# Cross-attention and FFN block on one core: where the feed-forward weights are converted, when they are loaded, and two early norms that read their root from PSUM

## Chip, cores, metric

The kernel runs on one core of one Trainium2 chip. The metric is device time in microseconds (us) of one execution. Three timed runs of the kernel before gave 454.68, 455.16 and 455.61 us; the median is 455.16.

## What is computed

Sixteen batches of 128 tokens and 512 features go through one cross-attention (32 query heads of 16, 8 groups of keys and values, so four query heads share a group) with a residual, and then a gated feed-forward in fp8 with a residual.

```python
def xattn(q, kv, Wq, Wk, Wv, Wfc, bfc):
    qh = heads(q @ Wq.T, 32)                    # q = layernorm(x)
    kh, vh = repeat(heads(kv @ Wk.T, 8), 4), repeat(heads(kv @ Wv.T, 8), 4)
    attn = softmax(qh @ kh.T / 4, axis=-1)
    return (attn @ vh) @ Wfc.T + bfc
def ffn(x, w_gating, w_linear):                 # operands cast to e4m3, results bf16
    return q8(gelu(q8(x) @ q8(w_gating[0])) * (q8(x) @ q8(w_gating[1]))) @ q8(w_linear)
x = x + xattn(layernorm(x), ctx, ...)
x = x + ffn(layernorm(x), ...)
```

`w_gating` is 2 x 512 x 2048 and `w_linear` 2048 x 512, both fp32 in memory. Before a matmul may use them they have to be clamped to +-240 and written as fp8.

## The kernel before

**Stages.** The batches go in eight pairs, p = 0 to 7 (`NB = 2`). Each pair has a softmax stage and an "up" stage. The softmax stage is a loop over slots n = 0 to 19: in slot n TensorE (PE) makes the transposed scores of tile n (L557, 16 tiles), ScalarE (ACT) takes two exponentials of them (`p`, L838, fp32, and `phi`, L841, fp16), GpSimd (POOL) subtracts (`plo`, L1277), and three slots later PE weighs the values with `plo` and `phi` (L577, L579). Between these, the same slots prepare pair q = p + 1: keys, values, the first norm `xn` (L1034), its transposition by PE (L497), the query projection (L451 to L453) and its split `cq` (ACT L824, VectorE (DVE) L1002). The up stage has eight units k = 0 to 7. It finds the row maxima of the next pair (PE L528, then DVE L1070), for p = 0 it runs the output projection of batch 0 (`bank<-wfc,aoT`), and for p >= 1 it runs the gating matmuls of pair p - 1 (L649) with their gelu and copy on ACT (L860, L864), product and fp8 clamp on DVE (L1126, L1136). The second norm `xn2` is L1120.

**What fills a tile by DMA.** The projected queries and keys are restacked by DMA: `qs<-cq` (L381, and L904 from ACT's queue in the first pair), `ks<-khl` (L367), `kmask<-khl` (L359), and the rows of maxima `qs<-mrow` (L387, and L893 from ACT's queue). The transposed scores wait for them. SP issues nearly all DMAs, in the order of its program; it stands still where a load has to wait for its place.

**The weights.** All weights are 29 chunks c of 512 KB: 0 to 4 are those of the attention, 5 to 20 the gating weights, 21 to 28 the linear ones. `W_PLACE` names the place into which chunk c is loaded (three stage buffers, `x4`/`x6` = rows of the residual's ring not yet used, `l`, `g` = the room of fp8 tiles that are written later). A chunk is converted in one of two ways: by one DVE instruction (L1016, the chunks in `W_DVE`, in the slots of `DVE_SLOTS`), or by a clamp on POOL (L1297) and a cast on ACT (L779), in the slots of `CLAMP_SLOTS` (cast two slots later) and the units of `CLAMPS_UP` (cast one unit later). `W_LOADS` says at which of four points of SP's program in p = 0 and p = 1 a chunk is loaded: after `kmask`, after the keys, the context and x, after the queries, and after the rows of maxima of the next pair.

```python
W_DVE = [7, 8, 9, 17, 18, 19, 20, 21, 22]
CLAMP_SLOTS = ((10,), ())
DVE_SLOTS = ((3, 6, 9), (2, 4, 6, 8, 11, 13))
CLAMPS_UP = (tuple(range(6)), (0, 1, 2, 4, 5, 6))
W_LOADS = (((), range(12, 18), (), range(18, 21)), ((), range(21, 26), range(26, CHUNKS), ()))
```

Every engine works through its own program in order, with semaphores between them. From pair 2 on no chunk is left, and a pair takes the same time as every other.

## Time and profile before

| | us |
|---|---|
| runs | 454.68, 455.16, 455.61 |
| profiled execution | 456.79 |
| its span | 454.80 |
| busy: PE, DVE, ACT, POOL | 424.9, 330.5, 313.8, 239.8 |
| mean granted TensorE clock | 0.966 of full speed |

```profile
## 2 busy tenths in 40 slices
PE   6887889799899999999999999999999998999997
PEld 6755756577677778787877778787877785568783
DVE  4776578888987589767897689758987676666351
ACT  6845958685798747974697748974698647865450
POOL 5575996694639702883168603983178502950000
PEclk9966958899999999999999999999999999999999
DMA  8894598286503370145303460236203330000001
```

One digit is the busy share of 11.4 us in tenths; PEclk is the TensorE clock granted. The first softmax stage lies in slices 3 to 6, its up stage in 6 and 7, the second pair in 7 to 11. After that the pattern repeats. Start times in the rows are us from the start of the span.

### The profile page before, as it was taken

The page shows a single profiled execution, that of the slowest core. Times are in us where ns is not written, and L with a number is a line of the kernel's source. Part 1 is how long each engine was busy: PE and PEld are TensorE (multiplying, and loading weights), DVE is VectorE, ACT ScalarE, POOL GpSimd, SP SyncE. Part 2 cuts the span into 40 slices and gives each one's busy share as a digit, 9 for nine tenths or more (in the row PEclk, how much of TensorE's full clock was granted, in tenths as well). Part 3 has the DMA queues.
Part 4 walks back from the last instruction along what each step waited for, and adds up shares of the span by engine and source line. Part 5 has one row for each costly group of instructions (what it writes and reads, how often), then busy time and mean ns, then how long its engine had stood idle before and what let it go on. Part 6 is the DMA issues. An engine that isn't in the chain of part 4 may idle for free.

```text
span 454.8 us, 9696 instructions
## 1 busy us (share of the span) xinstructions
PE 424.9 (93%) x3596; PEld 329.1 (72%) x3596; DVE 330.5 (73%) x687; ACT 313.8 (69%) x576; POOL 239.8 (53%) x228
## 2 busy tenths in 40 slices
PE   6887889799899999999999999999999998999997
PEld 6755756577677778787877778787877785568783
DVE  4776578888987589767897689758987676666351
ACT  6845958685798747974697748974698647865450
POOL 5575996694639702883168603983178502950000
PEclk9966958899999999999999999999999999999999
DMA  8894598286503370145303460236203330000001
GB/s 277 305 251 163 146 340 234 66 303 143 188 1 89 94 190 4 43 123 117 95 5 95 114 163 1 67 101 156 56 20 100 76 88 3 25 25 1 2 25 69
DMA packets 21231, 49.66 MB, mean 109 GB/s; under 512 B 4672, under 2 KB 5184, under 8 KB 21184
## 3 DMA queue, kind: packets, MB, share of 16 engines
q1 hardware_dynamic: 20828, 48.22, 37.2%
q10 hardware_dynamic: 356, 0.82, 0.6%
q8 instruction: 29, 0.48, 0.5%
q14 instruction: 18, 0.15, 0.1%
HBM read 23.86 MB, written 4.19 MB: 62 GB/s over the span
## 4 chain that ended last, share of the span: by engine, by line
PE 69%; DVE 15%; POOL 6%; ACT 4%; issue 3%; DMA 2%; ACTq 1%; POOLq 0%; DVEq 0%
PE bank L649 21%; PE bank L668 11%; PE bank L451 7%; PE bank L452 6%; PE bank L453 6%; PE bank L557 5%; DVE mneg L1070 4%; POOL plo L1277 4%; PE bank L528 4%; PE bank L486 2%; PE bank L577 2%; PE bank L579 2%; DMA qs<-cq 2%; DVE osum L1083 2%; PE bank L497 1%
## 5 line engine op out<-in xcount | busy, mean ns | idle before, releaser
L1277 POOL TENSOR_TENSOR plo<-p,phi 128x512 f16<-128x512 f32 x128 | 152.6, 1204 | 70.3 <-ACT phi L841 69.5
L649 PE MATMUL bank<-x2T,wgate 128*128 128x256 fp8e4 x1024 | 125.1, 273 | 0.0
L649 PEld LDWEIGHTS bank<-x2T,wgate 128*128 128x128 fp8e4 x1024 | 94.7, 98 | 22.0 <-issue 5.6
L1070 DVE TENSOR_REDUCE mneg<-bank 128x4 fp32r<-128x512 f32 x128 | 84.5, 684 | 16.1 <-PE bank L528 15.9
L838 ACT ACTIVATE p<-bank 128x512 f32<-128x512 f32 x128 | 77.6, 606 | 21.2 <-PE bank L557 20.3
L841 ACT ACTIVATE phi<-bank 128x512 f16<-128x512 f32 x128 | 77.5, 605 | 0.0
L864 ACT CAST ff<-bank 128x512 bf16<-128x512 f32 x64 | 37.5, 585 | 46.0 <-PE bank L649 46.0
L528 PE MATMUL bank<-kmask,cq 128*128 128x512 f32 x128 | 60.1, 495 | 4.6 <-DVE mneg L1070 3.0
L668 PE MATMUL bank<-wlin,act 128*128 128x512 fp8e4 x224 | 64.3, 378 | 0.0
L557 PE MATMUL bank<-qs,ks 98*128 98x512 f32 x128 | 55.3, 432 | 4.5 <-ACT phi L841 2.4
L860 ACT ACTIVATE gate<-bank 128x512 bf16<-128x512 f32 x64 | 38.2, 597 | 26.0 <-PE bank L649 25.9
L577 PEld LDWEIGHTS bank<-vt,plo 128*128 128x128 f16 x512 | 32.1, 98 | 28.9 <-issue 19.1
L577 PE MATMUL bank<-vt,plo 128*128 128x49 bf16 x512 | 45.9, 190 | 2.1 <-POOL plo L1277 1.2
L579 PE MATMUL bank<-vt,phi 128*128 128x49 bf16 x512 | 43.9, 186 | 0.0
L451 PE MATMUL bank<-cx,wq 128*128 128x256 f32 x112 | 39.8, 356 | 0.8 <-DVE cx L1002 0.8
L1126 DVE TENSOR_TENSOR prod<-gate,ff 128x512 bf16<-128x512 bf16 x64 | 30.2, 472 | 13.1 <-ACT ff L864 13.1
L1261 POOL TENSOR_TENSOR cx<-cin,cx 128x512 fp32r<-128x512 f32 x14 | 18.1, 1296 | 38.6 <-ACT cx L788 38.6
L1256 POOL TENSOR_TENSOR rstd<-var,half_neg 128x1 f32<-128x1 f32 x16 | 9.1, 569 | 55.3 <-DVE var L1113 55.3
L1083 DVE TENSOR_REDUCE osum<-bank 128x128 f32<-128x384 f32 x64 | 35.7, 557 | 2.2
L451 PE MATMUL bank<-wfc,aoT 128*128 128x512 f32 x64 | 31.5, 493 | 3.8 <-DVE aoT L1002 3.7
L579 PEld LDWEIGHTS bank<-vt,phi 128*128 128x128 f16 x512 | 33.4, 98 | 0.0
L528 PEld LDWEIGHTS bank<-kmask,cq 128*128 128x128 f32 x128 | 25.1, 201 | 10.3 <-DVE mneg L1070 6.6
(117 smaller groups left out, 823.1 us busy)
## 6 DMA issues: line engine op xcount, KB each, us to landing
qs<-cq SPq DMA_DIRECT2D x90, 128.0 KB, 2.4
stage<-in_w SPq DMA_DIRECT2D x15, 512.0 KB, 6.7
ks<-khl SPq DMA_DIRECT2D x96, 64.0 KB, 2.0
cin<-in_ctx SPq DMA_DIRECT2D x8, 512.0 KB, 4.1
xr<-in_x SPq DMA_DIRECT2D x16, 256.0 KB, 3.2
out<-xr SPq DMA_DIRECT2D x16, 256.0 KB, 2.5
raw_l<-in_w SPq DMA_DIRECT2D x4, 512.0 KB, 8.9
raw_g<-in_w SPq DMA_DIRECT2D x4, 512.0 KB, 9.6
```

The costliest lines, as they stand in the source:

```text
L451: pe.matmul(out, a[1], b[0], start=first, stop=False)
L528: pe.matmul(bank_of("S", q, i, s)[:, :], cq[:, 0, j, tok(i)], kmask[:, 2 * half:2 * half + 2, :, tok(i)], start=True, stop=True).then_inc( ...
L557: pe.matmul(T[n % 2][:, :], ks[rows, p % 2, g // 2, g % 2, tok(i)], qs[rows, g // 2, :, tok(i)], start=True, stop=True).then_inc(st_done, 1)
L577: pe.matmul(out, plo[:, (TILES * p + n) % PBUF, j * SEQ:(j + 1) * SEQ], vt[:, p % 2, i, g, :], start=True, stop=False)
L579: mm = pe.matmul(out, phi[:, (TILES * p + n) % PBUF, j * SEQ:(j + 1) * SEQ], vt[:, p % 2, i, g, :], start=False, stop=True)
L649: mm = pe.matmul(out[:, h * TOK:(h + 1) * TOK], wgate8[:, UH * v + h, kk, part, :], x2T[:, pair, kk, :], start=kk == 0, stop=kk == KT - 1)
L668: mm = pe.matmul(lin_bank(b)[:, :], act_tile(b // NB)[:, h, b % NB, :], wlin8[:, h, :], start=h == 0, stop=h == HT - 1)
L838: act.activation(p32[:, e % P32BUF, :], T[n % 2][:, :], ACT.Exp, scale=QUARTER).then_inc(p32_ok, 1)
L841: act.activation(phi[:, e % PBUF, :], T[n % 2][:, :], ACT.Exp, scale=QUARTER).then_inc(phi_ok, 1)
L1070: dve.tensor_reduce(dst[:, :, 2 * half:2 * half + 2, j].rearrange("p a r -> p r a"), bank_of("S", q, i, s)[:, :].rearrange("p (r a k) -> p ...
L1083: dve.tensor_reduce(osum[:, b, :].rearrange("p (h d) -> p h d", h=UHEADS), o[:, :, 0:VPARTS * HD].rearrange("p h (a d) -> p h d a", a=VPARTS),
L1277: pool.tensor_tensor(plo[:, e % PBUF, :], p32[:, e % P32BUF, :], phi[:, e % PBUF, :], ALU.subtract).then_inc(plo_ok, 1)
```

## The change

It is in five parts, all of them before pair 2.

1. The loads of chunks 7 to 11 wait on SP until all four parts of the first queries are stacked, and the DMA of the second batch's row maxima is issued between the third and the fourth of them.
2. In the first softmax stage DVE converts six chunks (7 to 12, in slots 5, 6, 7, 8, 9, 11) where it was three (slots 3, 6, 9); POOL and ACT still convert one, in slot 12 where it was slot 10. In the first up stage POOL and ACT convert five where it was six, in the second four (units 1, 2, 4, 5) where it was six (0, 1, 2, 4, 5, 6). DVE converts six in the second softmax stage, as before.
3. Chunks 12 to 14 are loaded right behind `kmask`; 21 and 22 only when the row maxima of pair 1 have landed (`m_stacked[0]`); 25 to 28 all behind the queries and x of pair 1's part of SP's program (25 was ahead of the queries).
4. For the first norm of pairs 1 and 2, and the second norm of batches 0 and 1, DVE first copies the root to a PSUM bank and takes it from there, by scalar_tensor_tensor in place of tensor_scalar.
5. PE's output projection of batches 0 and 1 waits until the norms of the pair whose root lies in its bank are done. DVE's first conversion of a linear chunk waits for places l0 and l1.

```diff
-W_PLACE += ["st0", "st1", "st2", "l0", "g0", "g1", "st0", "st1", "l1"]
-W_PLACE += ["st2", "x6", "st0", "st1", "st2", "st0", "st1", "st2"]
-W_DVE = [7, 8, 9, 17, 18, 19, 20, 21, 22]
+W_PLACE += ["st0", "st1", "st2", "x6", "l0", "g0", "g1", "l1", "st0"]
+W_PLACE += ["st1", "st2", "x6", "st0", "st1", "st2", "st0", "st1"]
+W_DVE = [7, 8, 9, 10, 11, 12, 19, 20, 21, 22, 23, 24]
-CLAMP_SLOTS = ((10,), ())
-DVE_SLOTS = ((3, 6, 9), (2, 4, 6, 8, 11, 13))
-CLAMPS_UP = (tuple(range(6)), (0, 1, 2, 4, 5, 6))
-W_LOADS = (((), range(12, 18), (), range(18, 21)), ((), range(21, 26), range(26, CHUNKS), ()))
+CLAMP_SLOTS = ((12,), ())
+DVE_SLOTS = ((5, 6, 7, 8, 9, 11), (2, 4, 6, 8, 11, 13))
+CLAMPS_UP = (tuple(range(5)), (1, 2, 4, 5))
+W_LOADS = ((range(W_FREE, 15), range(15, 21), (), range(21, 23)), ((), range(23, 25), range(25, CHUNKS), ()))
...
+        def root2(b):
+            return chain_banks(b)[1][:, NB:NB + 1]
...
             stack_q(0, PAIRS - 1)
+            for hp in range(PAIRS):
+                sp.wait_ge(q_stacked[hp], 16 * 3)
             for c in range(W_GATE + W_AHEAD, W_FREE):
+                if c == W_GATE + W_AHEAD + STAGES:
+                    stack_max(0, 1)
                 load_chunk(c)
...
+                if p == 0:
+                    sp.wait_ge(m_stacked[0], 32)
                 for c in W_LOADS[p][3] if p < 2 else ():
...
+                    if b < NB:
+                        pe.wait_ge(xn_ok, NB * (b + 2))
                     pe.wait_ge(aoT_lo, b + 1)
...
+                    root = G[q - 1][:, 0:NB]
+                    if i == 0:
+                        dve.wait_ge(*((aoT_lo, NB) if q == 2 else (max_ok, TILES)))
+                        dve.tensor_copy(root, rstd1[:, :]).then_inc(root1_ok, 1)
+                        dve.wait_ge(root1_ok, q)
+                    dve.scalar_tensor_tensor(xn[:, i, :], x0, mv1[:, i, 0:1], root[:, i:i + 1].broadcast_to([P, D]),
+                                             ALU.subtract, ALU.mult).then_inc(xn_ok, 1)
...
+                    dve.tensor_copy(root2(b), rstd2[:, i:i + 1]).then_inc(root2_ok, 1)
+                    dve.wait_ge(root2_ok, b + 1)
+                    dve.scalar_tensor_tensor(xn2[:, :], xr[:, b % RING, :], mv2[:, i, 0:1], root2(b).broadcast_to([P, D]),
+                                             ALU.subtract, ALU.mult, saturate=False).then_inc(xn2_ok, 1)
```

Line numbers move with the change: the DVE conversion is L1016 before and L1031 after, the norms L1034 and L1059, POOL's clamp L1297 and L1328, `plo` L1277 and L1308, a load of a chunk L338 and L341.

**SP's queue between the first queries and the keys of pair 1** (`xr`, `raw_l`, `raw_g`, `stage` are places of chunks). Before:

```order
L381 DMA qs<-cq 32x1024 x6
L338 DMA xr<-in_w 128x1024
L338 DMA raw_l<-in_w 128x1024
L338 DMA raw_g<-in_w 128x1024 x2
L338 DMA raw_l<-in_w 128x1024
L387 DMA qs<-mrow 2x16x128
L359 DMA kmask<-khl 32x512 x4
L367 DMA ks<-khl 32x512 x12
```

After:

```order
L384 DMA qs<-cq 32x1024 x6
L341 DMA xr<-in_w 128x1024
L341 DMA raw_l<-in_w 128x1024
L341 DMA raw_g<-in_w 128x1024
L390 DMA qs<-mrow 2x16x128
L341 DMA raw_g<-in_w 128x1024
L341 DMA raw_l<-in_w 128x1024
L362 DMA kmask<-khl 32x512 x4
L341 DMA stage<-in_w 128x1024 x3
L370 DMA ks<-khl 32x512 x12
```

The row maxima have passed two loads, and three stage loads now stand ahead of the keys.

**DVE in the middle of the first softmax stage** (`bank<-rstd` is the copy of the root, `wgate` a converted chunk). Before:

```order
L1034 TENSOR_SCALAR xn<-xr,mv,rstd 128x512 x2
L1016 TENSOR_SCALAR wgate<-xr 128x1024
L1002 TENSOR_TENSOR cx<-bank,cx 128x4x128
L1081 RECIPROCAL bank<-bank 128x8
L1083 TENSOR_REDUCE osum<-bank 128x128
L1002 TENSOR_TENSOR cx<-bank,cx 128x4x128
L1093 TENSOR_TENSOR ao<-osum,bank 128x128
L1016 TENSOR_SCALAR wgate<-raw_l 128x1024
```

After:

```order
L1057 COPY bank<-rstd 128x2
L1059 SCALAR_TENSOR_TENSOR xn<-xr,mv,bank 128x512 x2
L1014 TENSOR_TENSOR cx<-bank,cx 128x4x128
L1106 RECIPROCAL bank<-bank 128x8
L1108 TENSOR_REDUCE osum<-bank 128x128
L1014 TENSOR_TENSOR cx<-bank,cx 128x4x128
L1118 TENSOR_TENSOR ao<-osum,bank 128x128
L1031 TENSOR_SCALAR wgate<-xr 128x1024
L1031 TENSOR_SCALAR wgate<-raw_l 128x1024
```

The first conversion has left the place ahead of the split of `cx`, and stands with the second behind the first `ao`.

**POOL in the second up stage** (`plo` ends the softmax stage, `cx` is the split of a later pair's context). Before:

```order
L1277 TENSOR_TENSOR plo<-p,phi 128x512 x7
L1297 TENSOR_SCALAR stage<-stage 128x1024
L1285 TENSOR_TENSOR xr<-xr,bias 128x512 x2
L1256 TENSOR_TENSOR rstd<-var,half_neg 128x1
L1297 TENSOR_SCALAR stage<-stage 128x1024
L1261 TENSOR_TENSOR cx<-cin,cx 128x512
L1297 TENSOR_SCALAR stage<-stage 128x1024
L1261 TENSOR_TENSOR cx<-cin,cx 128x512
L1297 TENSOR_SCALAR stage<-stage 128x1024 x3
```

After:

```order
L1308 TENSOR_TENSOR plo<-p,phi 128x512 x7
L1316 TENSOR_TENSOR xr<-xr,bias 128x512 x2
L1287 TENSOR_TENSOR rstd<-var,half_neg 128x1
L1328 TENSOR_SCALAR stage<-stage 128x1024
L1292 TENSOR_TENSOR cx<-cin,cx 128x512
L1328 TENSOR_SCALAR stage<-stage 128x1024
L1292 TENSOR_TENSOR cx<-cin,cx 128x512
L1328 TENSOR_SCALAR stage<-stage 128x1024 x2
```

The first clamp now is that of chunk 25, directly behind the root of the second norm; before it was the second of the stage, and of chunk 24.

## Rows read from the trace of the kernel before

**Rows 1.** Windows by stage: us, busy by engine (instructions), PEclk, DMA share, GB/s

```profile
29.26:74.83 45.57, 38.48 (x265) 29.56 (x266) 29.63 (x61) 33.47 (x56) 33.08 (x31) 0.73 0.76 228
74.83:130.59 55.76, 49.52 (x437) 39.52 (x436) 49.72 (x96) 41.84 (x77) 36.06 (x32) 0.97 0.53 163
180.90:231.30 50.40, 49.90 (x448) 39.30 (x446) 39.81 (x85) 36.44 (x70) 26.87 (x25) 1.00 0.33 85
```

**Rows 2.** Chain of waits from 24 to 132 us: start, us, what

```profile
28.59 7.41 DMA qs<-cq
...
71.74 3.27 DVE mneg L1070 x5
...
80.29 2.03 DVE xn L1034 x2
...
82.92 1.29 DVE xn L1120
```

**Rows 3.** Timeline of PE, 34 to 65 us: start, us, what [idle before <- releaser]

```profile
36.05 0.50 PE L557 MATMUL bank<-qs,ks 98*128 98x512 f32 x1 [1.90 <-DMA qs<-cq]
36.38 1.65 PE L486 MATMUL bank<-wv,cx 128*128 128x256 f32 x8
...
39.40 1.12 PE L497 MATMUL bank<-ident,xn 128*128 128x128 f32 x4 [0.59 <-DVE xn L1034]
...
62.39 1.05 PE L595 MATMUL bank<-ident,ao 128*128 128x128 f32 x4
```

**Rows 4.** Timeline of SP's queue

```profile
27.68 0.59 SPq L338 DMA_DIRECT2D xr<-in_w  x1
...
58.04 11.58 SPq L381 DMA_DIRECT2D qs<-cq  x12
...
113.79 5.12 SPq L338 DMA_DIRECT2D stage<-in_w  x3
```

**Rows 5.** Timeline of POOL and ACT in the first softmax stage

```profile
42.85 1.16 POOL L1277 TENSOR_TENSOR plo<-p,phi 128x512 f16<-128x512 f32 x1 [2.04 <-ACT phi L841]
...
44.59 1.62 POOL L1277 TENSOR_TENSOR plo<-p,phi 128x512 f16<-128x512 f32 x1
...
48.20 4.99 POOL L1277 TENSOR_TENSOR plo<-p,phi 128x512 f16<-128x512 f32 x4
...
60.18 1.04 POOL L1297 TENSOR_SCALAR raw_l<-raw_l 128x1024 f32<-128x1024 f32 x1
...
54.22 1.06 ACT L779 ACTIVATE wgate<-raw_g 128x1024 fp8e4<-128x1024 f32 x1 [0.36 <-POOL raw_g L1297]
```

**Rows 6.** Windows of 3.4 us, columns as in rows 1

```profile
53.70:57.10 3.40, 1.99 (x22) 1.13 (x20) 1.42 (x4) 3.04 (x7) 3.01 (x4) 1.00 0.94 289
57.20:60.60 3.40, 3.35 (x36) 2.18 (x36) 3.30 (x9) 3.38 (x5) 3.40 (x4) 0.50 0.95 324
...
81.00:84.40 3.40, 1.48 (x21) 1.01 (x18) 3.40 (x5) 1.27 (x4) 2.62 (x2) 1.00 0.20 49
84.50:87.90 3.40, 3.21 (x17) 2.52 (x18) 2.92 (x8) 2.24 (x5) 1.85 (x2) 0.50 0.37 87
```

**Rows 7.** DMA to landing of the `qs<-cq` transfers (L381) issued from 58.0 to 59.2

```profile
DMA to landing us min/median/max: 9.6/9.7/12.2
```

**Rows 8.** Timeline of DVE: operations with a PSUM operand, and a conversion

```profile
42.45 0.20 DVE L1081 RECIPROCAL bank<-bank 128x8 f32<-128x8 f32 x1
...
77.11 0.67 DVE L1107 TENSOR_TENSOR xr<-xr,bank 128x512 f32<-128x512 f32 x1
...
84.47 0.68 DVE L1016 TENSOR_SCALAR wgate<-stage 128x1024 fp8e4<-128x1024 f32 x1
```

**Rows 9.** Timeline of the second up stage: DVE, ACT, POOL

```profile
114.46 1.49 DVE L1126 TENSOR_TENSOR prod<-gate,ff 128x512 bf16<-128x512 bf16 x1
...
116.04 0.60 ACT L860 ACTIVATE gate<-bank 128x512 bf16<-128x512 f32 x1
...
118.47 1.08 POOL L1297 TENSOR_SCALAR stage<-stage 128x1024 f32<-128x1024 f32 x1 [0.22 <-DMA stage<-in_w]
```

More of the change, by code:

```diff
@@ L242, in xattn_ffn_kernel @@
         aoT_done, aoT_hi, aoT_lo, fc_done = sem("aoT_done"), sem("aoT_hi"), sem("aoT_lo"), sem("fc_done")
-        x1_ok, stat2, mv2_ok, var2_ok, rstd2_ok, xn2_ok, x2T_done, x2T_ok = (
+        x1_ok, stat2, mv2_ok, var2_ok, rstd2_ok, xn2_ok, x2T_done, x2T_ok, root1_ok, root2_ok = (
             sem("x1_ok"), sem("stat2"), sem("mv2_ok"), sem("var2_ok"), sem("rstd2_ok"), sem("xn2_ok"),
-            sem("x2T_done"), sem("x2T_ok"))
+            sem("x2T_done"), sem("x2T_ok"), sem("root1_ok"), sem("root2_ok"))
         gate_done, ff_done, ff_ok, gelu_ok, prod_ok, act_ok = (
@@ L414, in _ @@
                 downs = down_slots(p)
-                stack_max(p, 1)
+                if p:
+                    stack_max(p, 1)
                 if q < NP:
@@ L1015, in chunk @@
                 dve.wait_ge(*chunk_in(c))
+                if c == W_LIN:
+                    for name in ("l0", "l1"):
+                        dve.wait_ge(*chunk_free(last_of(name)))
                 dve.tensor_scalar(chunk_fp8(c), chunk_place(c), FP8_MAX, -FP8_MAX, ALU.min, ALU.max,
@@ L1033, in norm_apply @@
                     dve.wait_ge(xT_done, NB * (q - 1) + i + 1)
-                dve.tensor_scalar(xn[:, i, :], xr[:, (NB * q + i) % RING, :], mv1[:, i, 0:1], rstd1[:, i:i + 1],
-                                  ALU.subtract, ALU.mult).then_inc(xn_ok, 1)
+                x0 = xr[:, (NB * q + i) % RING, :]
+                if q == 0 or q > 2:
+                    dve.tensor_scalar(xn[:, i, :], x0, mv1[:, i, 0:1], rstd1[:, i:i + 1],
+                                      ALU.subtract, ALU.mult).then_inc(xn_ok, 1)
+                else:
+                    root = G[q - 1][:, 0:NB]
[4 more added lines that the diff above has]
+                    dve.scalar_tensor_tensor(xn[:, i, :], x0, mv1[:, i, 0:1], root[:, i:i + 1].broadcast_to([P, D]),
+                                             ALU.subtract, ALU.mult).then_inc(xn_ok, 1)
             def context_low(q, h):
@@ L1119, in norm2_apply @@
                     dve.wait_ge(x2T_done, b)
-                dve.tensor_scalar(xn2[:, :], xr[:, b % RING, :], mv2[:, i, 0:1], rstd2[:, i:i + 1],
-                                  ALU.subtract, ALU.mult, saturate=False).then_inc(xn2_ok, 1)
+                if b >= NB:
+                    dve.tensor_scalar(xn2[:, :], xr[:, b % RING, :], mv2[:, i, 0:1], rstd2[:, i:i + 1],
+                                      ALU.subtract, ALU.mult, saturate=False).then_inc(xn2_ok, 1)
+                else:
+                    dve.tensor_copy(root2(b), rstd2[:, i:i + 1]).then_inc(root2_ok, 1)
+                    dve.wait_ge(root2_ok, b + 1)
+                    dve.scalar_tensor_tensor(xn2[:, :], xr[:, b % RING, :], mv2[:, i, 0:1], root2(b).broadcast_to([P, D]),
+                                             ALU.subtract, ALU.mult, saturate=False).then_inc(xn2_ok, 1)
             def product(u):
```

## The prediction

> **What bounds the kernel now.** I read the windows by stage first. A pair without conversions takes 50.40 us, with PE busy 49.90 of it at full clock; the first pair's 45.57 us have PE busy only 38.48, at a mean clock of 0.73, and the second pair takes 55.76 us [rows 1]. PE bounds the rest of the run, where nothing is changed, so whatever the change brings or costs lies before 130.6 us and reaches the end one for one. Then the chain of waits from 24 to 132 us. With the timelines beside it, it shows five places that the change touches. (a) The second part of the queries, issued at 28.59, lands 7.41 us later [rows 2]; PE stands idle 1.90 us for it [rows 3]. SP began five chunk loads at 27.68, in the middle of that transfer [rows 4]. (b) From 42.85 on POOL's `plo` is the chain, 1.16 us each, with a clamp among them. ACT's cast at 54.22 waited for that clamp and holds ACT for 1.06 us [rows 5]; the split of the queries comes after it, and PE, which needs the split for its scores, is busy only 1.99 of 3.40 us [rows 6]. (c) Behind that gap the granted clock falls from 1.00 to 0.50 [rows 6], which is from 2.4 to 1.2 GHz, and the clock line of the page has it low in the slices up to about 71 us, over PE's out-projection. (d) At 80.29 two norms take 2.03 us and at 82.92 one takes 1.29, DVE's last work before PE may go on [rows 2]. (e) In the second up stage a product on DVE takes 1.49 us beside POOL's clamps [rows 9].
>
> **Part 1, the held loads.** With no chunk in the queue I expect the query DMAs to land by PE's need, so the 1.90 us of idle go. The value projection behind it ran at half clock, 1.65 us for eight [rows 3]; with the idle gone PE may be at full clock there and in the transposition (1.12 us). I take half of the projection's possible 0.8, because ACT's two exponentials end no earlier, and half of 1.12 for the transposition, 0.5. Part 4 takes some back: the norm that starts this step (two operations at about half a microsecond each) becomes a copy of 0.20 and operations of 0.67, by the nearest rows with a PSUM operand [rows 8], +0.35 to the first. Sum -1.9 - 0.4 - 0.5 + 0.35 = **-2.4** at POOL's `plo` of 42.85. Both ends: 0, if the queries themselves are the traffic, and -3.0.
>
> **Part 2, conversions.** In the part where POOL is the chain, two DVE conversions became dear for it: one `plo` took 1.62 in place of 1.16 (+0.46), and four took 4.99 in place of 4.64 (+0.35) [rows 5]. Now there are six, so four more at 0.4: +1.6. Below, nothing, if they fall into gaps; above, the whole 0.68 that a conversion takes by itself [rows 8], 4 x 0.68 = 2.7. I take 0.4, since it is the same pair of instructions side by side. The clamp stays one, but in slot 12, so the idle of 0.4 that POOL had behind ACT's cast goes. POOL, done at 60.18 [rows 5], is then done at 60.2 - 2.4 + 1.6 - 0.4 = 59.0. The last weighing, reciprocal, sum and division (0.4 + 0.2 + 0.55 + 0.3) put PE's turn of the output at 60.4, where it was 62.39 [rows 3]: **-2.0**. DVE comes out about there too: its split of the queries no longer waits for a cast of 1.06, which gives its last 7.6 us of work a start 2.4 + 1.0 earlier, less the delay that POOL passes on.
>
> The Trainium skill's page "Advanced Engine Details and Errata" (VectorE Performance Modes, Mode Summary) speaks against this part: the second SBUF port of VectorE is shared with GpSimd, and two-port VectorE instructions and GpSimd's block each other. Read as a full block it gives the upper end, +2.7; the `plo` rows show about 60% of that.
>
> **The clock in the first up stage.** PE's idle in the window from 53.7 was the wait for the split. Without it the fall at 57.2 should not come at that place. The out-projection at full clock would shorten the 12.6 us from the turn (62.39) to the end of the maxima (71.74 + 3.27) by 3.4 us, since DVE waits for PE's scores there. That is not free to reach the end: the query DMAs of pair 1 need 9.6 to 12.2 us to land, on DMA engines that are full (share 0.94 and 0.95 from 53.7 to 60.6) [rows 6, 7]. Their order and start hardly move (SP at 58.04 [rows 4], now about 57.8). The first pair of tiles needs three of them, issued by 59.2 and landed by 71.4 at the latest, where the stage began at 74.83 [rows 1]. Through the keys and their split the norms then move by at most 2.1 us more. But a pause of its own follows the turn (ACT and DVE split it before PE projects), and windows with some such idle did lower the clock [rows 6]. Ends 0 and -2.1; I take **-1.0**, a fall that comes one or two windows later. One cast fewer (six to five) costs and gives nothing here: DVE and DMA end last.
>
> **Part 4, second pair.** The two norms of 2.03 become 0.20 + 2 x 0.60 = 1.4 (PSUM operations of 0.67 follow each other every 0.60), the one of 1.29 becomes 0.15 + 0.65 = 0.8: -1.1. A conversion between them lay in a gap of POOL's at 0.68; shifted, it may take 0.2 more. **-0.9**, ends 0 and -1.2. PE's out-projection of batch 1 now waits for these norms, 0.65 us later; behind it stands the next scores tile. PE is idle for more than that before the transposition that follows (1.48 busy of 3.40 [rows 6]), which covers it; without that cover it would cost its 0.65. The clock was at half from 84.5 to 87.9, behind a stretch with PE busy 1.48 of 3.40 us [rows 6]; with 0.9 less of that idle it may hold. Ends 0 and -1.2, taken **-0.3**, the idle being only half gone. `plo` loses one blocked neighbour: **-0.2**.
>
> **Part 3, the second up stage.** Chunk 25 was loaded ahead of the queries. Now it is the first of the loads behind them. The load that stood there, issued at 113.79, was what POOL waited for before its clamp of 118.47 [rows 4, 9]. So in the old time frame the clamp of chunk 25 runs 118.5 to 119.5, behind it on POOL the context and all other clamps; its cast stands on ACT ahead of the gelu of unit 3, which ran at 116.04 [rows 9] and comes to 119.5 + 1.0 + 0.55 = 121.1, 5.0 later. PE may run two units ahead of ACT, and two casts are gone from ACT. Its work from 121.1 on is five gelus, five copies, a transposed tile and the maxima, 5.8 us, three casts, 3.0, and the table load and first exponential's start, 1.4: 131.3, where the next stage began at 130.59 [rows 1]. For DVE's tail I add 0.2. On the other side DVE is rid of the contention around 114 to 117 (1.49 us for a product [rows 9]). That gain ends in the same wait. **+0.9**; ends 0, if PE and DVE are late anyway, and +5.0. The loads of 21 and 22 wait for the maxima, but are used in slots 6 and 8 of the next stage: nothing.
>
> **Sum:** -2.0 - 1.0 - 0.9 - 0.3 - 0.2 + 0.9 = -3.5 us. The profiled execution took 456.79 (span 454.80, and 1.99 around it), 1.63 over the median of 455.16. So 453.3 in a profiled run and **451.7** as a median.
>
> **Rivals.** *B, the clock holds.* If the pause after the turn does not lower it, and the one at 84 neither: -2.0 - 2.1 - 0.9 - 0.7 - 0.2 + 0.9 = -5.0, 450.2. For it: the page's clock line shows no fall at the same place of the second pair (103 to 107). Against: there the gating matmuls fill in. *C, POOL swallows it.* Conversions block `plo` in full, +2.7, and delay the sums before PE: the first term shrinks to -0.6; with the clock as before, -0.6 - 0.9 - 0.2 + 0.9 = -0.8, 454.4. This is the skill's rule as a mechanism; for it, that PE and POOL work at the same pace there; against it, the +0.35 to 0.46 of the rows. *E, the hold does nothing.* The queries' own 1.5 MB keep the DMA engines busy before any load starts, so the 1.90 us stay: -1.6, 453.6. *D, slower.* The wait for chunk 25 passes whole, +5.0 in place of +0.9, and PE, idle for some 3 us as in 81.0 to 84.4, falls to half clock for a window of units, +1.3 more: +1.9, 457.1. It decides as soon as PE's two units of lead are used up before ACT's cast; a landing over 4.6 us after the issue brings that on.
>
> **Numbers.** Forecast 0.42, B 0.25, C 0.13, D 0.10, E 0.10. A measurement of this kernel can tell about 0.2%, 0.9 us, from no change. Faster by more: the forecast, B, most of E and a third of C, 0.78. Within 0.2%: the rest of C and E and a bit of D, 0.13. Slower 0.09. The range reaches from below B, 449.4, to C's far side, 454.5; what it leaves out is D and the tails of B.
>
> **What would show it.** Right: the idle before the third L557 under 0.3 us; POOL's last `plo` of the stage at 58 to 60; the turn at 60 to 61; norms of 0.6 to 0.7 us each at pair 2; POOL waiting some 4 us for a stage DMA at the second up stage, and ACT's cast behind it. Wrong: more than 0.6 us for POOL per conversion (C), a granted clock of 1.00 all through the out-projection (B), the second pair longer than 56 us (D), or an idle of 1.9 us for `qs<-cq` still there (E).

## The result, and the profile after

The changed kernel takes 457.76 us (median of 20 runs) beside 455.65 of the kernel before, a ratio of **1.0046, 95% interval 1.0026 to 1.0065**: 2.1 us slower, where 451.7 was forecast and 454.5 was the upper end. Its profiled execution took 457.00 us, span 455.2. The ratios leave out runs in a slower state of the chip, which makes that of e1 below the least certain: three of the four left out there (458.8 to 461.4 us) lie close above the slowest one kept (458.7), and with these three its median is 457.2 and not 455.6.

The two profiled executions differ by less than the medians: that of the kernel before took 456.79 us, 1.1 over its median of these runs, that of the changed kernel 457.00, 0.8 under. The stages below therefore account for 0.3 us of the 2.1; the other 1.8 can't be placed in a stage.

Windows by stage of the changed kernel (columns as in rows 1; its stages begin at 71.85, 102.74 and 130.92):

```profile
29.26:71.85 42.59, 33.21 (x265) 24.80 (x266) 33.45 (x66) 32.44 (x56) 33.71 (x30) 0.88 0.86 270
71.85:102.74 30.89, 27.05 (x271) 21.93 (x270) 27.13 (x59) 23.80 (x49) 25.86 (x23) 0.94 0.43 130
102.74:130.92 28.18, 23.33 (x162) 18.05 (x159) 18.95 (x39) 15.54 (x26) 7.42 (x7) 0.88 0.50 142
130.92:181.30 50.38, 49.88 (x448) 39.31 (x446) 39.82 (x84) 36.45 (x71) 26.87 (x25) 1.00 0.34 86
```

The first pair ends at 71.85, where it ended at 74.83 [rows 1]: 3.0 us gained. They are still there when the second up stage begins (102.74, before 105.87), and gone when it ends (130.92, before 130.59). So the up stage of the second pair took 28.2 us in place of 24.7 and gave back 3.5. The pairs behind it are unchanged (50.38 and 50.40 us).

Timeline of PE in the changed kernel, 32 to 60 us, beside [rows 3]:

```profile
32.37 0.50 PE L567 MATMUL bank<-qs,ks 98*128 98x512 f32 x1
32.71 1.11 PE L496 MATMUL bank<-wv,cx 128*128 128x256 f32 x8
...
36.49 0.65 PE L507 MATMUL bank<-ident,xn 128*128 128x128 f32 x4 [2.23 <-DVE xn L1059]
...
59.50 1.05 PE L605 MATMUL bank<-ident,ao 128*128 128x128 f32 x4
```

The idle of 1.90 before the third scores tile is gone, which comes 3.7 us sooner. The value projection is at full clock (1.11 for 1.65). PE then waits 2.23 us for the norm, where it was 0.59 [rows 3], and so the transposition comes 2.9 us sooner.

The second up stage in the changed kernel (timeline), beside [rows 4, 9]:

```profile
110.92 8.35 SPq L341 DMA_DIRECT2D stage<-in_w  x4
...
116.78 1.04 POOL L1328 TENSOR_SCALAR stage<-stage 128x1024 f32<-128x1024 f32 x1 [6.68 <-DMA stage<-in_w]
117.86 1.06 ACT L791 ACTIVATE wlin<-stage 128x1024 fp8e4<-128x1024 f32 x1 [7.05 <-POOL stage L1328]
...
119.33 0.59 ACT L872 ACTIVATE gate<-bank 128x512 bf16<-128x512 f32 x1
120.06 1.87 PE L661 MATMUL bank<-x2T,wgate 128*128 128x256 fp8e4 x8 [4.78 <-ACT gate L872]
120.98 0.59 DVE L1157 TENSOR_TENSOR prod<-gate,ff 128x512 bf16<-128x512 bf16 x1 [6.20 <-ACT ff L876]
122.16 1.93 PE L661 MATMUL bank<-x2T,wgate 128*128 128x256 fp8e4 x8
...
125.59 1.05 PE L661 MATMUL bank<-x2T,wgate 128*128 128x256 fp8e4 x8
```

This is read from the left column down (a unit has two rows of eight gating matmuls, one for its gelu and one for its copy): SP issues the load of chunk 25 at 110.92; POOL clamps it at 116.78, after 6.68 us with nothing to do; ACT casts it at 117.86, and only then comes the gelu of unit 3 (119.33, before 116.04 with everything in front of it 3.1 us later). PE had used up its lead: unit 5 may not begin before the gelu of unit 3, and PE waited 4.78 us for it. The windows of 3.4 us show what that does to the clock:

```profile
110.70:114.10 3.40, 3.40 (x31) 2.73 (x29) 3.31 (x8) 0.11 (x1) 0.00 (x0) 1.00 0.97 249
114.10:117.50 3.40, 1.18 (x10) 0.78 (x8) 0.68 (x1) 0.00 (x0) 0.71 (x1) 1.00 0.89 337
117.50:120.90 3.40, 0.84 (x5) 0.62 (x6) 0.00 (x0) 3.04 (x6) 3.40 (x4) 0.54 0.34 124
120.90:124.30 3.40, 3.40 (x15) 2.19 (x13) 3.26 (x5) 2.68 (x6) 2.75 (x3) 0.50 0.17 66
124.30:127.70 3.40, 3.40 (x28) 2.78 (x27) 2.90 (x6) 2.88 (x5) 0.00 (x0) 0.95 0.01 4
```

Behind 3.4 us with PE busy 1.18 the granted clock is 0.54 and then 0.50 (1.2 of 2.4 GHz), and the two rows of unit 5 take 1.87 and 1.93 us, where a row takes 1.05 later in the stage.

### The profile page after: what moved, and what is told of

It is laid out like the page before. It is cut to its first block, busy times and chain, and to the rows that moved or that the text cites. A ratio compares the mean times of both kernels' runs of the same rounds, so it can differ in the third digit from the quotient of the medians.

```text
span 455.2 us, 9703 instructions
## 1 busy us (share of the span) xinstructions
PE 422.3 (93%) x3596; PEld 327.0 (72%) x3596; DVE 332.4 (73%) x694; ACT 310.5 (68%) x573; POOL 237.8 (52%) x225
## 4 chain that ended last, share of the span: by engine, by line
PE 67%; DVE 11%; POOL 6%; SPq 5%; ACT 5%; DMA 4%; issue 2%; ACTq 1%; POOLq 0%; DVEq 0%
PE bank L661 20%; PE bank L680 11%; PE bank L461 6%; PE bank L462 6%; PE bank L463 6%; PE bank L567 5%; PE bank L538 4%; POOL plo L1308 4%; DVE mneg L1095 3%; PE bank L496 2%; PE bank L587 2%; SPq L384 2%; SPq L370 2%; PE bank L589 2%; DVE osum L1108 2%
## 5 line engine op out<-in xcount | busy, mean ns | idle before, releaser
L1308 POOL TENSOR_TENSOR plo<-p,phi 128x512 f16<-128x512 f32 x128 | 153.2, 1211 | 66.1 <-ACT phi L853 65.3
L661 PE MATMUL bank<-x2T,wgate 128*128 128x256 fp8e4 x1024 | 127.0, 276 | 4.8 <-ACT gate L872 4.8
L567 PE MATMUL bank<-qs,ks 98*128 98x512 f32 x128 | 53.9, 421 | 2.4 <-ACT phi L853 1.7
L872 ACT ACTIVATE gate<-bank 128x512 bf16<-128x512 f32 x64 | 38.2, 597 | 24.7 <-PE bank L661 24.6
L461 PE MATMUL bank<-cx,wq 128*128 128x256 f32 x112 | 39.8, 356 | 1.8 <-DVE cx L1014 1.8
L589 PEld LDWEIGHTS bank<-vt,phi 128*128 128x128 f16 x512 | 32.7, 97 | 0.0
L462 PE MATMUL bank<-cx,wq 128*128 128x256 f32 x112 | 31.5, 281 | 0.0
```

The lines of the kernel that those rows point to most:

```text
L461: pe.matmul(out, a[1], b[0], start=first, stop=False)
L462: pe.matmul(out, a[0], b[1], start=False, stop=False)
L567: pe.matmul(T[n % 2][:, :], ks[rows, p % 2, g // 2, g % 2, tok(i)], qs[rows, g // 2, :, tok(i)], start=True, stop=True).then_inc(st_done, 1)
L589: mm = pe.matmul(out, phi[:, (TILES * p + n) % PBUF, j * SEQ:(j + 1) * SEQ], vt[:, p % 2, i, g, :], start=False, stop=True)
L661: mm = pe.matmul(out[:, h * TOK:(h + 1) * TOK], wgate8[:, UH * v + h, kk, part, :], x2T[:, pair, kk, :], start=kk == 0, stop=kk == KT - 1)
L1308: pool.tensor_tensor(plo[:, e % PBUF, :], p32[:, e % P32BUF, :], phi[:, e % PBUF, :], ALU.subtract).then_inc(plo_ok, 1)
```

## The experiments

Every ratio is to runs of the kernel before in the same session, with its 95% interval; 0.001 is 0.46 us. The three columns behind it come from one profiled execution each: when the second softmax stage, the second up stage and the third pair begin. From one execution to another of kernels that are alike up to there, such a start moves by 1 us or so (the first column lies between 71.85 and 73.5 for all kernels with the changed conversions), so single differences under 1 us are not read. The difference of two ratios of this table is uncertain by 1.3 to 2.2 us.

| kernel | ratio | softmax 2 | up 2 | pair 3 |
|---|---|---|---|---|
| before | 1 | 74.8 | 105.9 | 130.6 |
| changed | 1.0046 [1.0026, 1.0065] | 71.9 | 102.7 | 130.9 |
| e1_25_ahead | 0.9981 [0.9938, 1.0024] | 73.0 | 105.7 | 129.2 |
| e2_before_25_behind | 1.0022 [0.9989, 1.0054] | 75.7 | 108.0 | 133.2 |
| e3_no_roots | 1.0019 [0.9988, 1.0050] | 73.5 | 106.5 | 132.8 |
| e4_no_hold | 1.0079 [1.0048, 1.0109] | 72.8 | 103.5 | 131.6 |
| e5_later_clamps | 1.0012 [0.9983, 1.0041] | 73.1 | 103.9 | 128.6 |
| e6_23_early | 0.9949 [0.9928, 0.9969] | 73.4 | 103.8 | 127.2 |
| e7_before_hold | 0.9956 [0.9934, 0.9978] | 70.1 | 101.4 | 126.1 |
| e8_no_clamp_softmax | 1.0058 [1.0031, 1.0085] | 72.3 | 104.7 | 131.7 |
| e9_hold_roots | 0.9984 [0.9958, 1.0009] | 71.0 | 103.8 | 128.4 |
| e10_25_before_x | 1.0001 [0.9973, 1.0030] | 73.0 | 105.5 | 129.2 |
| e11_hold_roots_early | 0.9913 [0.9880, 0.9946] | 72.1 | 101.2 | 126.8 |
| e12_no_roots_early | 0.9972 [0.9947, 0.9997] | 72.5 | 104.2 | 127.6 |
| e13_hold_early | 0.9948 [0.9911, 0.9984] | 69.7 | 99.5 | 124.3 |
| e14_only_23_early | 0.9995 [0.9970, 1.0020] | 72.2 | 101.4 | 127.8 |

**The load of chunk 25 (e1, e2, e10, e5).** The first puts it back:

```
-W_LOADS = (..., ((), range(23, 25), range(25, CHUNKS), ()))
+W_LOADS = (..., ((), range(23, 26), range(26, CHUNKS), ()))
```

> The changed kernel with one load put back: chunk 25 is loaded ahead of the queries of pair 2 again, as it was before the change. Theory D (the late landing of chunk 25 is what ate the gain): POOL's clamp in the second up stage starts with no DMA wait, PE's idle of about 4 us there and the half clock behind it are gone, some DVE contention comes back; the next stage starts 2 to 3.5 us sooner than in the changed kernel, and the whole is 0 to 1.5 us below the kernel before (changed kernel: 2.1 above it). Rival (the loss sits elsewhere, in the conversions or in the order of DVE, and the wait is only where it shows): the up stage ends no more than 1 us sooner, and the whole stays 1 to 2 us above the kernel before.

Measured: 3.0 us below the changed kernel (0.9981 against 1.0046, uncertain by 2.1) and 0.9 below the kernel before, which is inside its interval. The total alone doesn't carry the theory; the stage does. The up stage shrank from 28.2 to 23.5 us (129.2 - 105.7), but the softmax stage in front of it grew from 30.9 to 32.7, so that the next stage began 1.7 us sooner and not 2 to 3.5. The timeline of DVE in the softmax stage shows why:

```profile
95.23 0.69 DVE L1031 TENSOR_SCALAR wlin<-xr 128x1024 fp8e4<-128x1024 f32 x1 [3.49 <-DMA xr<-in_w]
...
98.73 1.10 DVE L1031 TENSOR_SCALAR wlin<-stage 128x1024 fp8e4<-128x1024 f32 x1 [1.10 <-DMA stage<-in_w]
```

DVE waits 4.6 us for chunks 23 and 24. In the changed kernel it waits 1.50 for chunk 23, and in the kernel before it already waited 1.15 at the same slot, for chunk 21 (98.02). That is a second late landing, of which the prediction said nothing.

The same move, alone on the kernel before (`range(21, 25), range(25, CHUNKS)` in place of `range(21, 26), range(26, CHUNKS)`):

> The kernel before with only the load of chunk 25 moved behind the queries of pair 2. Its clamp there is the third of the stage (unit 2), not the first of four (unit 1), in an up stage that starts 3.1 us later. Theory D: POOL waits for the landing 5 us or more after the issue at about 113, ACT's cast waits behind it, PE idles and falls to half clock: 3 to 5 us slower than the kernel before. Rival (a load behind the queries costs little by itself, since before the change POOL waited for one there too without harm to PE): within 1 us of the kernel before.

Measured: 1.0 us slower, interval -0.5 to +2.5, nearer to the rival than to the 3 to 5 us expected. There the chunk is the third one clamped, in unit 2. So the load behind the queries is not dear by itself: it is dear together with a clamp of it in unit 1. The other half of that pair was then changed alone, with the loads as in the changed kernel:

```
-CLAMPS_UP = (tuple(range(5)), (1, 2, 4, 5))
+CLAMPS_UP = (tuple(range(5)), (2, 4, 5, 6))
```

> The changed kernel with the clamps of the second up stage one unit later: units 2, 4, 5, 6 in place of 1, 2, 4, 5; the loads stay where the change put them. If what costs is ACT's cast of chunk 25 standing ahead of the gelu of unit 3 while the chunk is under way, then moving it one unit lets one more unit pass before the wait: PE's idle there shrinks by about one unit (2 us or so), the up stage takes 26 to 27 us in place of 28.2, and the total is 1 to 2 us below the changed kernel. Rival (the landing of the chunk is all that matters, the last casts now come too late for the end of the stage): no shorter than the changed kernel, or longer.

Measured: 1.5 us below the changed kernel (uncertain by 1.6); the up stage took 24.7 us (expected 26 to 27), and ACT waited 3.71 us before its cast in place of 7.05. With one more unit of gelus in front of the cast the stage is as short as before the change (24.7), with the loads of the changed kernel.

Then the landing itself, with chunk 25's load still behind the queries, but before the two loads of x:

```
+                if p == 1:
+                    load_chunk(25)
                 if p and q + 1 < NP:
                     load_x(q + 1)
...
```

> The changed kernel with the load of chunk 25 still behind the queries of pair 2, but issued before the two loads of x (512 KB together) in place of after them. Theory (the landing sets the up stage, and it is made of SP's issue time and of the bytes ahead of it): issued 1.1 to 1.4 us sooner and with 512 KB less in front, it lands 2 to 3 us sooner, at about 114; POOL's wait shrinks from 6.7 to about 4 us, the up stage from 28.2 to 26 us, and the total is 1 to 2.5 us below the changed kernel, near the kernel before. Rival (the 1.5 MB of the queries fill the DMA engines, the x loads are no obstacle): landing less than 1 us sooner, total as the changed kernel.

Measured: 2.1 us below the changed kernel (uncertain by 1.6), as expected, though the wait shrank further than to 4 us. Timeline of SP and POOL:

```profile
110.08 1.10 SPq L341 DMA_DIRECT2D stage<-in_w  x1
...
114.57 1.04 POOL L1331 TENSOR_SCALAR stage<-stage 128x1024 f32<-128x1024 f32 x1 [2.00 <-DMA stage<-in_w]
```

From issue to clamp 4.49 us, where it was 5.86 behind the loads of x. The stage itself began 2.8 us later in this run, so that POOL came to the clamp nearer to the landing; the up stage took 23.7 us (expected 26), with a wait of 2.00 about as short as that of e1 without one before this clamp (23.5).

Taken together, the up stage took 26.2 to 28.2 us in the five kernels that clamp chunk 25 in unit 1 with its load behind the queries and x (changed, e3, e4, e8, e14), and 23.3 to 24.7 in the five others with the changed conversions (e1, e5, e6, e10, e12).

**The wait for chunks 23 and 24 (e6, e14).** Chunk 23 is loaded with 21 and 22 (`range(21, 24)` in the first pair's last list), before the keys of pair 1 are stacked; e6 has chunk 25 ahead of the queries as well, e14 has not.

> The changed kernel with chunk 25 loaded ahead of the queries of pair 2, as in the first of these runs, and chunk 23 loaded with chunks 21 and 22 at about 71 us, before the keys of pair 1 are stacked, in place of at 90. In the run with chunk 25 alone, DVE waited 4.6 us for chunks 23 and 24, which were then the second and third of four transfers in a row, and the second softmax stage was 1.8 us longer than in the changed kernel. Theory (two landings bound the second pair, each where it is first wanted): the wait for chunk 23 is gone, DVE waits 1 us or less, the second softmax stage takes 30.5 to 31.5 us and the up stage 23 to 24.5; the next stage begins at about 127 to 128, and the total is 2 to 4 us below the kernel before. Rival (PE's work in the softmax stage or POOL's products bound it anyway): the stage stays at 32 or more and the total is within 1 us of the run with chunk 25 alone.

> The changed kernel with chunk 23 loaded at about 72 instead of 90, chunk 25 left behind the queries as the change has it. Theory (two late landings, and the later one decides): DVE's wait of 1.5 us in the second softmax stage goes and that stage ends 0.5 to 1.5 us sooner, but the clamp of chunk 25 then waits as long after an issue that moves along with the queries, so that the up stage stays at 27 to 28.5 us with PE idle and at half clock: total 0 to 1.5 us below the changed kernel, still above the kernel before. Rival (the wait for chunk 23 was the main loss): total 2 us or more below the changed kernel.

Measured: e6 is 2.3 us below the kernel before and 4.4 below the changed kernel; DVE has no wait for a load, the softmax stage took 30.4 us, the up stage 23.4. With chunk 23 alone early, e14 is 2.3 us below the changed kernel, more than the 0 to 1.5 expected, and what its rival had said (2 or more): softmax stage 29.2 us with a wait of 0.37 left to DVE, up stage 26.4, POOL waiting 5.41. So of 4.4 us some 2 lie at each of the two landings. How they add up can't be read closer than the intervals of these differences, 1.3 to 2.1 us.

Why the chunks are late shows in the chain of waits of the changed kernel, 76 to 95 us:

```profile
76.87 0.25 ACT mrow L843
77.14 0.68 SPq L390
...
80.47 0.54 SPq L370
...
89.20 0.58 SPq L355
89.78 0.04 issue
89.83 4.42 DMA xr<-in_w
94.27 1.30 DVE wlin L1031
```

SP can't issue the row of maxima of batch 1 before 77.14. Behind it stand four masks, twelve copies of keys (8.7 us of issuing) and the context; the load of chunk 23 comes 12.7 us later. In the kernel before the same row went out at 81.06 and the first chunk behind it at 93.61, 12.5 us later. So the load moved up with that row, by 3.8 us, and nothing that DVE or POOL gains behind the row moves it further. In this stretch of the changed kernel the chain is SP's queue; in the kernel before it is mostly POOL's `plo` from 88 us on.

**The hold (e4, e7).** Taken out of the changed kernel (the two lines with `sp.wait_ge(q_stacked[hp], 16 * 3)`), and put into the kernel before (the same two lines ahead of the loads of chunks 5 to 11):

> The changed kernel with the loads of chunks 5 to 11 not held for the queries of pair 0 (the wait is taken out, all else as in the changed kernel). Theory (the hold brought 2.9 us at the first transposition, 1.9 of idle and 1.0 of half clock): the third tile L567 comes at about 36 instead of 32.4, the first softmax stage and everything to the second up stage 2.5 to 3 us later, and the total 2.5 to 3 us above the changed kernel. Rival (something later sets the pace, above all the DMA engines, so that the 2.9 us are not passed on): under 1.5 us above the changed kernel.

> The kernel before with the hold alone: the loads of chunks 5 to 11 wait until the queries of pair 0 are stacked. Theory: 2.5 to 3 us gained at the third scores tile, and since here the order of loads, clamps and conversions is that of before, nothing takes it back: the second softmax begins 2 to 3 us sooner and the total is 2 to 3 us below the kernel before. Rival (the second up stage always meets its loads late, since SP's queue sets them, so that any gain in front of it is lost): the second up stage is longer by as much, total within 0.9 us of the kernel before.

Measured: without it the changed kernel is 1.5 us slower (interval of that difference about -0.1 to 3.2), below the 2.5 to 3 expected and at the edge of the rival; its third scores tile came at 34.89 behind 0.80 us of idle, so the 3.7 us between 36.05 and 32.37 are not all the hold's. Alone on the kernel before it brings 2.0 us (1.0 to 3.0), as expected. The second softmax stage there begins at 70.1, 4.7 us sooner than before and sooner than in any kernel with the changed conversions.

**The clock and the cast (e8).** `CLAMP_SLOTS = ((), ())` and a sixth clamp in the first up stage.

> The changed kernel with no clamp in the first softmax stage: the clamp of slot 12 goes into the up stage behind it, which has six clamps then, as before the change. Theory (the cast of 1.06 us behind that clamp on ACT made PE idle and so the clock fall at about 57): POOL's last plo ends about 1 us sooner, PE has no idle of over 1 us between 53 and 56, and the granted clock stays at 1.00 to 60 or longer; the second pair's first tile, which waits for a DMA issued after the maxima of batch 0, comes 0.5 to 2 us sooner. Rival (the clock falls anyway in the pause at the turn of the output): clock half from about 60 on, second pair at most 0.5 us sooner. In the total both are at most half visible, since the second up stage takes gains back in the changed kernel.

Measured: same as the changed kernel within the noise (1.0058). The granted clock did hold up to 70 us: windows of 2 us of this kernel,

```profile
62.00:64.00 2.00, 2.00 (x10) 1.66 (x11) 1.38 (x2) 1.01 (x3) 2.00 (x3) 1.00 1.03 399
64.00:66.00 2.00, 1.57 (x7) 0.86 (x5) 1.64 (x3) 0.87 (x2) 2.00 (x3) 1.00 1.01 367
66.00:68.00 2.00, 1.30 (x3) 0.37 (x2) 2.00 (x4) 2.00 (x3) 2.00 (x3) 1.00 1.06 282
68.00:70.00 2.00, 0.00 (x0) 0.00 (x0) 1.97 (x7) 1.55 (x2) 0.46 (x1) 1.00 1.07 259
70.00:72.00 2.00, 0.48 (x1) 0.41 (x2) 1.55 (x4) 0.00 (x0) 0.00 (x0) 0.57 0.98 244
```

where the changed kernel has 0.50, 0.50, 0.85, 1.00 and 1.00 in the same windows. But the second pair began no sooner (72.35, changed 71.85). In the chain of waits of this run,

```profile
62.56 8.91 DMA qs<-mrow
71.47 0.04 issue
71.52 0.79 PE bank L567
```

and in that of the changed kernel:

```profile
64.63 6.64 DMA qs<-mrow
71.27 0.04 issue
71.31 0.51 PE bank L567
```

The row of maxima, 16 KB, was issued 2.1 us sooner and landed 0.2 us later: it goes through DMA engines with a busy share of 1.0 or over, behind the queries and the loads. PE, at full clock, stood idle from 68 to 70 for it. Behind that idle the clock was lost: 0.57, 0.50 and 0.50 from 70 to 76 us, where the changed kernel has 1.00. So this run shows what sets the start of the second pair; what a clock that holds on both sides of the start is worth in the total it can't show.

**The roots in PSUM (e3, e9, e12, e11 with e13).** e3 takes them (and PE's wait) out of the changed kernel; e9 is the kernel before with the hold and the roots; e12 is e6 without roots; e13 is the kernel before with the hold and chunks 21 and 22 loaded with 18 to 20, and e11 is e13 with the roots.

> The changed kernel with the norms of pairs 1 and 2 and of the first two batches as before, their reciprocal roots read from SBUF, and without the wait of PE's out-projection for the norms. Theory (the roots in PSUM brought what was counted for them, about 0.9 us in front of pair 2, and what they brought was swallowed by the wait for chunk 25): the norms of pair 2 take about 2.0 us in place of 1.4, the queries of pair 2 come 0.5 to 1 us later, the second up stage ends at the same time within 0.5 us as long as the landing of chunk 25 moves too, so the total is 0.5 to 1 us above the changed kernel. Rival (the copies into PSUM and PE's new wait cost as much as the norms gain): same as the changed kernel or faster.

> Parts 1 and 4 alone: the kernel before with the hold of the loads of chunks 5 to 11 and with the roots in PSUM (and PE's wait for the norms); conversions, clamps and the order of all other loads as before the change. The hold alone measured 0.9956 of the kernel before. Theory (the roots bring about 0.9 us in front of pair 2 when no late load takes it back): 2.5 to 3.5 us below the kernel before, and 4.5 to 5.5 us below the changed kernel, which is then what the moved conversions, clamps and loads cost together. Rival (the roots bring nothing even so, since PE's new wait or POOL's products take it): the same as the hold alone, 2 us below.

> The run with chunk 23 early and chunk 25 ahead of the queries (0.9949 of the kernel before), without the roots in PSUM and without PE's wait for the norms. It is the fourth corner beside the hold alone (0.9956), hold and roots, and hold, roots and conversions. Theory: without the roots the norms of pair 2 take 2.0 us in place of 1.4, the start of pair 2's queries is 0.5 to 1 us later, total 0.5 to 1.5 us above the run with them. Rival (roots bring nothing): the same within 0.5 us.

> The run with the hold and the roots (conversions and clamps of before the change), with chunks 21 and 22 loaded behind chunks 18 to 20 at about 68 us in place of at 90. In the run with the hold alone DVE waited 1.8 us for chunk 21 in the second softmax stage. Theory (what an early load of a conversion's chunk brought there it brings here too): that wait is gone, the second softmax stage 0.5 to 1.5 us shorter, total 3 to 4.5 us below the kernel before, the fastest of all. Rival (five loads at 68 us lie on the landing of the queries or of the keys of the next pair, or the wait was hidden): no faster than without.

> The hold alone with chunks 21 and 22 loaded behind 18 to 20, and without the roots in PSUM: the fastest run so far (0.9913 of the kernel before) less the roots. In the run with hold and roots, DVE waited 3.0 us for the first chunk of the row loaded at 90, with the hold alone 1.8 us, and the roots brought nothing there. Theory (the roots' gain is real but ended in that wait): with the wait gone it shows, and this run is 0.5 to 1.5 us above the run with roots, at 0.993 to 0.996. Rival (the roots are worth nothing in the total): within 0.5 us of the run with roots, 0.990 to 0.992.

Measured, with roots less without: +1.2, +1.3, -1.0 and -1.6 us, each uncertain by 1.5 to 2.2. The first two (e3, e9) are nearer to what the rivals said, the last two to the theories of e12 and e13. The mean is zero; what the roots bring in the total stays open. In the records the two norms take 1.40 in place of 2.11, and the next 0.75 in place of 1.37. In one of the two comparisons where they seem to cost, DVE's wait for the first late chunk is this in e7 (hold alone, timeline of DVE):

```profile
93.29 0.95 DVE L1018 TENSOR_SCALAR wlin<-stage 128x1024 fp8e4<-128x1024 f32 x1 [1.83 <-DMA stage<-in_w]
```

and with the roots, in e9:

```profile
94.87 1.11 DVE L1023 TENSOR_SCALAR wlin<-stage 128x1024 fp8e4<-128x1024 f32 x1 [3.04 <-DMA stage<-in_w]
```

The wait is 1.2 us longer with the roots. In the other comparison both kernels wait 1.50 us (the changed kernel and e3). The first fits a gain that ends in the wait, and in the two comparisons without that wait (chunks loaded early) the roots come out ahead; but four differences of this size and noise don't show it.

e11 is the fastest of all, 4.0 us (2.5 to 5.5) below the kernel before and 6.1 below the changed kernel; e13 is 2.4 us below (0.7 to 4.1).

## Why the prediction was wrong

**The step that failed is Part 3**, "+0.9; ends 0 [...] and +5.0": measured, the second up stage grew from 24.7 to 28.2 us, **+3.5**. The working behind it names what happened, engine by engine: the clamp of chunk 25 behind the landing, ACT's cast ahead of the gelu of unit 3. Two of its sizes were too small. The first is the landing: the text took it from the load of 113.79, clamped 4.7 us after its issue; chunk 25 was clamped 5.9 us after. The gelu of unit 3 came at 119.33, which is 122.5 in the old frame (3.13 added), 6.4 later than before and 1.4 later than the forecast 121.1. The second is the way from that gelu to the next stage. The text counted 10.2 us of ACT's own work ("131.3, where the next stage began at 130.59") and left PE out; it took 11.6 (119.33 to 130.92). PE had three units and the scores between them to do, began at half clock and had no slack (busy 3.40 of 3.40 us in both windows behind 120.9). In the kernel before the same unit 5 began so (timeline of PE):

```profile
120.94 1.03 PE L649 MATMUL bank<-x2T,wgate 128*128 128x256 fp8e4 x8
```

and 9.65 us later came the next stage. In the changed kernel unit 5 began at 120.06, 2.25 later in the old frame, and the rest of the stage took 10.86, 1.2 longer: 3.5 in all. In the chain of waits the two rows of unit 5 stand with 1.87 and 1.73 in place of 0.89.

e1 and e10 shorten the stage by 4.5 to 4.7 us through the place of the load alone, e5 by 3.5 through the clamps alone.

**Rival D** named this place and this mechanism ("a landing over 4.6 us after the issue brings that on") and got 0.10. Its total, 457.1, lies near the measured 457.76 by luck: it priced the stage at +5.0 and +1.3, 6.3 us in place of 3.5, and took from the forecast gains in front of it that did not all come.

**The sum.** With 3.5 in place of 0.9 the forecast's -3.5 is -0.9. The stages in front brought 3.1 us in place of 4.4, which makes it +0.3, as the two profiled executions have it. The medians differ by 2.1; the remaining 1.8 no profile here places.

**Part 1**, -2.4 at POOL's `plo` of 42.85: measured -3.5 (39.38), of which clock more than was forecast. Right in kind; e7 shows a gain of the hold in the total, 2.0 us (1.0 to 3.0).

**Part 2**, +1.6 for POOL and -0.4 for its idle: POOL went from 17.33 us (42.85 to 60.18), busy 16.71 of them, to 18.57 (39.38 to 57.95), busy 18.36. That is 1.65 us more work for four more conversions in this part, 0.41 each, and 0.4 less idle: the price was right. The turn came at 59.50, -2.9. But the part counted POOL alone. "Their order and start hardly move (SP at 58.04 [...] now about 57.8)" was right too (57.82), and was a cost that the sum never carried: with the hold alone (e7) SP begins the queries of pair 1 at 55.50. From the row of maxima to these queries SP took 17.0 us before (41.05 to 58.04) and 17.1 in e7, and 20.3 in the changed kernel (37.57 to 57.82): two loads stand directly behind the row now and three ahead of the keys, some 2.8 us of issuing together. In the four kernels with the hold and the old conversions and loads (e7, e9, e11, e13) the second softmax stage begins at 69.7 to 72.1, mean 70.7; in the nine with the hold and the changed ones at 71.9 to 73.5, mean 72.8. These 2 us, from one execution each, were paid out of the hold's gain. Whether SP's queue or the DMA engines' load carries them was not separated.

The Trainium skill's page "Advanced Engine Details and Errata" (VectorE Performance Modes, Mode Summary) has two-port VectorE instructions and GpSimd's block each other. The rows agree in kind: 0.41 us more of POOL for each conversion, about 60% of the 0.68 that one takes alone.

**The clock in the first up stage**, -1.0: the first pair ended 3.0 us sooner, of which 2.9 was there at the turn, so the clock brought 0.1. "Without it the fall at 57.2 should not come at that place" rested on an idle that was still there: the cast of the one clamp left in the softmax stage began at 54.65, PE was busy 0.63 of 2.00 us from 54 to 56, and the clock was 0.59 from 56 to 58 and 0.50 up to 66. Windows of 2 us of the changed kernel:

```profile
54.00:56.00 2.00, 0.63 (x14) 0.33 (x11) 1.54 (x4) 1.35 (x2) 2.00 (x3) 1.00 0.96 366
56.00:58.00 2.00, 1.48 (x17) 0.78 (x13) 1.41 (x4) 1.98 (x3) 2.00 (x3) 0.59 0.92 221
```

In e8, without that clamp, PE was busy 1.37 from 54 to 56 and the clock stayed at 1.00. That this would start the second pair sooner, the 2.1 us of rival B (for which the text has no working), e8 speaks against: the landing of the row of maxima set the start all the same. The text had seen the full DMA engines but priced the queries' landing and not the 16 KB behind them.

**Part 4**, -0.9: the norms came out as forecast (1.40 and 0.75), and the fourth step gained about as much at the end of the norms (-4.1 us there, against -3.0 at the start of the stage). At the end of the softmax stage -3.1 was left. The two losses stand in DVE's rows: the conversion of chunk 23 began at 94.27, 3.75 sooner than the one in its place before (98.02), since its load had moved up by no more than 3.8; and it took 1.30 us in place of 0.69, so that the last splits of the queries came 3.1 sooner. The prediction counted the loads of 21 and 22 and not those of 23 and 24, which stand behind SP's queue.

Rivals: C asked for over 0.6 us of POOL per conversion, it was 0.41; E for an idle of 1.9 that had stayed, it was gone. Both are out.

## What to carry to other kernels

When a change gains time, list every load that a later stage waits for and ask what sets its issue: a load behind a long row of transfers in one queue moves up only with the event that starts the row, and what the engines gain behind that event ends in the wait for the load. Price a wait by what is queued in order behind it, on every engine (here a cast ahead of a gelu on ACT, then PE's lead of two units, its remaining work and its clock), not by the slack of one engine. And before a faster engine is counted, check whether the stage ends in a transfer through full DMA engines: here a clock at twice the speed did not start the next stage sooner.

## What the runs showed of the hardware

- A transfer of 16 KB took 6.64 us and, issued 2.1 us sooner, 8.91 us to land while the DMA engines' busy share was about 1.0. The query transfers of 128 KB issued from 60 to 76 us took 8.0 us in the median, where all of them have a median of 2.4: the landing went by what the engines had to do more than by the size.
- A load of 512 KB took 4.42 us as the second of three such transfers in a row (changed kernel), and 7.94 us as the third of four (e1); moving two loads of 256 KB from in front of one brought its clamp 1.4 us nearer to its issue.
- The granted clock fell from 1.00 to 0.54 behind one stretch of 3.4 us with PE busy 1.18, while in e8 it stayed at 1.00 over windows of 2 us with PE busy 2.00, 1.57, 1.30 and 0.00, and fell to 0.57 in the window after, with PE busy 0.48.
- The start of a stage with nothing changed in front of it moves by about 1 us between profiled executions (71.85 in the changed kernel, 72.98 in e1), as much as most terms of the prediction's sum.
